# A gated cross-attention block in fp32: GpSimd's mixes in quarters behind VectorE's splits, and a new order around the last product

## The reference

```python
x = x + tanh(g_xattn) * attention(layernorm(x), ctx)   # 32 heads of 128, 8 key/value heads, RMS-normed q and k, out @ Wo
flat = layernorm(x)
probs = softmax(flat @ router_w.T + router_b); topv, topi = top_k(probs, 2)
w     = zeros(N, 8) with gates topv / sum(topv) at topi
h     = einsum('nd,erd->ner', flat, A)                 # 8 experts of rank 16
x = x + tanh(g_ffn) * einsum('ner,eor->no', h * w[:, :, None], Bm) * 0.5
```

## Time and profile before

| | us |
|---|---|
| median of 3 runs (1689.0 to 1690.82) | 1689.81 |
| profiled execution | 1685.8 |
| its span | 1684.0 |
| TensorE busy | 1650.3 |
| VectorE busy | 1176.9 |
| GpSimd busy | 889.1 |
| ScalarE busy | 877.3 |

### The profile page before, as it was taken

One profiled execution on the slowest core, in us unless ns is written; L12 is line 12 of the kernel. 1 busy time (PEld: TensorE's weight loads), 2 busy tenths in 40 slices (PEclk: granted clock), 3 DMA queues, 4 the chain that ended last, 5 costly groups with the idle time before them and its releaser, 6 DMA issues.

```text
span 1684.0 us, 26179 instructions
## 1 busy us (share of the span) xinstructions
PE 1650.3 (98%) x9120; PEld 1470.7 (87%) x9120; DVE 1176.9 (70%) x2054; ACT 877.3 (52%) x1663; POOL 889.1 (53%) x700
## 2 busy tenths in 40 slices
PE   7999999999999999999999999999999999999997
PEld 6788888678888879999999999999999889999995
DVE  7788886677777752677677777776766777556676
ACT  5545554544544431566666666666666666443432
POOL 1344443134434420777777777777776455563131
PEclk9999999999999999999999999999999999999999
DMA  5567778736566647556666666655556566687551
GB/s 200 157 171 235 232 207 249 194 112 188 151 180 164 159 161 235 173 166 208 197 213 198 198 204 189 191 190 180 182 171 205 187 215 218 229 281 248 222 178 58
DMA packets 238503, 323.87 MB, mean 192 GB/s; under 512 B 53300, under 2 KB 193396, under 8 KB 233380
## 3 DMA queue, kind: packets, MB, share of 16 engines
q1 hardware_dynamic: 237796, 315.65, 60.3%
q10 hardware_dynamic: 576, 6.55, 1.0%
HBM read 212.18 MB, written 109.97 MB: 191 GB/s over the span
## 4 chain that ended last, share of the span: by engine, by line
PE 89%; DVE 6%; ACT 3%; issue 2%; DMA 0%; POOL 0%; DVEq 0%; SPq 0%; ACTq 0%; POOLq 0%
PE bank L991 26%; PE bank L993 25%; PE bank L992 25%; PE bank L1129 5%; PE bank L1096 2%; PE bank L1025 1%; PE bank L1335 1%; DVE wo_lo L2024 1%; DVE mx L2004 1%; DVE at_lo L2026 1%; ACT pr L1611 1%; ACT w_hi L1427 1%; PE bank L1346 0%; DMA wr<-Wkv 0%; DVE pT_lo L1998 0%
## 5 line engine op out<-in xcount | busy, mean ns | idle before, releaser
L911 POOL TENSOR_SCALAR pr<-pr,rr 100x461 f32<-100x461 f32 x256 | 371.1, 1457 | 162.1 <-DVE rr L2019 162.1
L991 PE MATMUL bank<-w_hi,a_hi 128*128 128x512 f32 (+1 forms) x856 | 341.2, 399 | 11.0 <-DVE a_lo L1794 8.5
L993 PE MATMUL bank<-w_hi,a_lo 128*128 128x512 f32 (+1 forms) x856 | 335.2, 392 | 0.0
L992 PE MATMUL bank<-w_lo,a_hi 128*128 128x512 f32 (+1 forms) x856 | 334.3, 391 | 0.0
L1611 ACT ACTIVATE pr<-bank,nm,rq 100x461 f32<-100x461 f32 x256 | 188.7, 737 | 156.7 <-DVE nm L2010 155.0
L2004 DVE TENSOR_REDUCE mx<-bank 100x1 f32<-100x461 f32 x256 | 161.4, 631 | 78.5 <-PE bank L993 75.2
L865 POOL TENSOR_TENSOR msk<-ssk,epst 128x4 f32<-128x4 f32 (+1 forms) x60 | 22.9, 382 | 348.4 <-DVE ssk L1825 348.4
L991 PEld LDWEIGHTS bank<-w_hi,a_hi 128*128 128x128 f32 (+1 forms) x856 | 157.8, 184 | 48.4 <-issue 9.6
L993 PEld LDWEIGHTS bank<-w_hi,a_lo 128*128 128x128 f32 (+1 forms) x856 | 157.6, 184 | 38.4
L991 PE MATMUL bank<-xT_hi,wq_hi 128*128 128x400 f32 x512 | 188.3, 368 | 0.7 <-issue 0.7
L992 PEld LDWEIGHTS bank<-w_lo,a_hi 128*128 128x128 f32 (+1 forms) x856 | 158.0, 185 | 34.7
(11 more groups left out here) (159 smaller groups left out, 3556.1 us busy)
## 6 DMA issues: line engine op xcount, KB each, us to landing
kT_d<-kst SPq DMA_DIRECT2D x56, 512.0 KB, 5.6
v_d<-vst SPq DMA_DIRECT2D x56, 512.0 KB
kT<-kT_d SPq DMA_DIRECT2D x64, 361.0 KB, 4.5
kvr<-ctxT SPq DMA_DIRECT2D x44, 512.0 KB, 5.9
wq_raw<-Wq SPq DMA_DIRECT2D x32, 512.0 KB, 5.8
tb<-Wo SPq DMA_DIRECT2D x16, 1024.0 KB, 8.5
wt_d<-tb SPq DMA_DIRECT2D x16, 1024.0 KB, 7.8
wo_raw<-wt_d SPq DMA_DIRECT2D x16, 1024.0 KB, 7.4
```

What stands on the lines that cost most here:

```text
L911: pool.tensor_scalar(pr[0:NQ, u % 2, i], pr[0:NQ, u % 2, i], rr[0:NQ, i:i + 1], None, ALU.mult).then_inc(p_done, 1)
L991: pe.matmul(o, lh, rh, start=start, stop=False, skip_group_check=more)
L992: pe.matmul(o, lh, rl, start=False, stop=False, skip_group_check=more)
L993: return pe.matmul(o, ll, rh, start=False, stop=stop, skip_group_check=more)
```

## The change

GpSimd's three mixes become three sets of four instructions of 400 columns. Ahead of each set stands a wait for the split of a chunk (17, 18 and 19), and the counts of `mix_done` follow (3 becomes 12, 4 becomes 13). TensorE's c0 and d0 stand behind turn_y(3), ahead of the last product's last halves. For that c takes banks 4 and 0 and d takes 5 and 1, batch 7 has a tile of its own for `x1` (so it needn't wait for the end of batch 3), `halves_to` counts all first halves before the second ones, and the load of batch 7's input stands ahead of the store of batch 2. VectorE does d0's residual and two of the last four additions ahead of the routing's top, and a1's residual ahead of batch 3's gates.

```diff
+        x1_last = at("x1_last", RAW + 8 * KB, [P, D])
 def out_bank(t, half):
-            return ((4, 0), (5, 1), (4, 5), (0, 1))[t - TB][half] if t >= TB else 4 + half
+            return ((4, 0), (5, 1), (4, 0), (5, 1))[t - TB][half] if t >= TB else 4 + half
+        def x1_of(t):
+            return x1_last[:] if t == B - 1 else x1[:, t % 4]
 def halves_to(t, half):
-            return 1 + ((0, 0), (1, 0), (2, 0), (0, 1), (1, 1), (2, 1), (3, 0), (3, 1)).index((t - TB, half))
+            return 1 + t - TB + TB * half
 SyncE
             next_res(2)
+            next_res(3)
             store(2)
-            next_res(3)
 GpSimd
             pool.wait_ge(oT_dve, 10)
             pool.wait_ge(oT_act, 6)
-            pool.tensor_tensor(oT_late[:, first], oT_late[:, first], oT_early[:, second], ALU.add).then_inc(mix_done, 1)
-            pool.tensor_tensor(oT_early[:, second], oT_early[:, second], oT_late[:, second], ALU.add).then_inc(mix_done, 1)
-            pool.wait_ge(mix_done, 2)
-            pool.tensor_tensor(oT_late[:, second], oT_late[:, second], oT_late[:, first], ALU.add).then_inc(mix_done, 1)
+            pool.wait_ge(wo_lo_done, split_after(FIRST_OF[P4] + 1))
+            for c in range(GQ):
+                pool.tensor_tensor(oT_late[:, c], oT_late[:, c], oT_early[:, GQ + c], ALU.add).then_inc(mix_done, 1)
+            pool.wait_ge(wo_lo_done, split_after(FIRST_OF[P4] + 2))
+            for c in range(GQ, C):
+                pool.tensor_tensor(oT_early[:, c], oT_early[:, c], oT_late[:, c], ALU.add).then_inc(mix_done, 1)
+            pool.wait_ge(wo_lo_done, split_after(FIRST_OF[P4] + 3))
+            pool.wait_ge(mix_done, 2 * GQ)
+            for c in range(GQ, C):
+                pool.tensor_tensor(oT_late[:, c], oT_late[:, c], oT_late[:, c - GQ], ALU.add).then_inc(mix_done, 1)
 TensorE, turn_half
+                if t < TB + 2 and half == 0:
+                    pe.wait_ge(x1_done, 2 * TB)
+                if t >= TB + 2:
+                    pe.wait_ge(x1_done, 2 * TB + halves_to(t - 2, half))
+                if t == TB and half == 0:
+                    pe.wait_ge(oT_dve, 16)
+                    pe.wait_ge(mix_done, 3 * GQ + 1)
 TensorE, turn_y
                 if t > TB + 1:
-                    pe.wait_ge(x1_done, 2 * TB + halves_to(t, 1))
+                    pe.wait_ge(x1_done, 2 * TB + halves_to(TB + 3, t - TB - 2))
 TensorE, order
                 if n == 4 * GQ - 3:
                     turn_half(a, 0)
                     turn_half(b, 0)
+                if n == 4 * GQ - 2:
+                    turn_half(c, 0)
+                    turn_half(d, 0)
             last_half(0)
             last_half(1)
             low_rank(TB - 1)
-            turn_half(c, 0)
             last_half(2)
             last_half(3)
...
             low_rank(a)
-            turn_half(d, 0)
             turn_half(d, 1)
 VectorE, residual_half
-                    dve.wait_ge(x2_done, 2 * (t - 4) + 2)
+                    if t < B - 1:
+                        dve.wait_ge(x2_done, 2 * (t - 4) + 2)
 VectorE, last_accumulators(some) adds the banks in `some` only
 VectorE, order
             residual_half(b, 0)
+            residual_half(c, 0)
+            residual_half(d, 0)
+            last_accumulators((0, 1))
             route_top(TB - 1)
-            residual_half(c, 0)
-            last_accumulators()
+            last_accumulators((2, 3))
+            residual_half(a, 1)
             route_gates(a - 1)
-            residual_half(a, 1)
             residual_half(b, 1)
             final(a - 1)
             residual_half(c, 1)
             route(a)
-            residual_half(d, 0)
             residual_half(d, 1)
```

More of the change, by code:

```diff
@@ L960, in _ @@
                 chunk_sums(m)
-            first, second = (slice(0, C // 2), slice(C // 2, C))
             pool.wait_ge(oT_dve, 10)
             pool.wait_ge(oT_act, 6)
-            pool.tensor_tensor(oT_late[:, first], oT_late[:, first], oT_early[:, second], ALU.add).then_inc(mix_done, 1)
-            pool.tensor_tensor(oT_early[:, second], oT_early[:, second], oT_late[:, second], ALU.add).then_inc(mix_done, 1)
-            pool.wait_ge(mix_done, 2)
-            pool.tensor_tensor(oT_late[:, second], oT_late[:, second], oT_late[:, first], ALU.add).then_inc(mix_done, 1)
+            pool.wait_ge(wo_lo_done, split_after(FIRST_OF[P4] + 1))
[8 more added lines that the diff above has]
+                pool.tensor_tensor(oT_late[:, c], oT_late[:, c], oT_late[:, c - GQ], ALU.add).then_inc(mix_done, 1)
             for t in range(B):
@@ L1734, in norm @@
                     act.wait_ge(t2_done, t - 1)
-                act.activation(y[0:NQ, t % 2], x1[0:NQ, t % 4], ACT.Identity, bias=mv2[0:NQ, t, 3:4],
+                act.activation(y[0:NQ, t % 2], x1_of(t)[0:NQ], ACT.Identity, bias=mv2[0:NQ, t, 3:4],
                                scale=mv2[0:NQ, t, 1:2]).then_inc(y_done, 1)
@@ L2043, in accumulators @@
                 if o in (P4, P3):
-                    dve.wait_ge(mix_done, 3)
+                    dve.wait_ge(mix_done, 3 * GQ)
                 for n in (0, 1) if o in (P1, P7, P5, P2) else range(4):
@@ L2142, in residual @@
                 for n in range(2):
-                    dve.scalar_tensor_tensor(out=x1[0:NQ, t % 4, n * 512:(n + 1) * 512], in0=ps[out_bank(t, n)][0:NQ, :],
+                    dve.scalar_tensor_tensor(out=x1_of(t)[0:NQ, n * 512:(n + 1) * 512], in0=ps[out_bank(t, n)][0:NQ, :],
                                              scalar=gates_t[0:NQ, 0:1], in1=xr[t % 4][0:NQ, n * 512:(n + 1) * 512],
@@ L2147, in residual @@
                     dve.wait_ge(x1_done, 2 * t + n + 1)
-                    dve.bn_stats(bn6[0:NQ, t % 4, n], x1[0:NQ, t % 4, n * 512:(n + 1) * 512]).then_inc(st2_done, 1)
+                    dve.bn_stats(bn6[0:NQ, t % 4, n], x1_of(t)[0:NQ, n * 512:(n + 1) * 512]).then_inc(st2_done, 1)
                 dve.wait_ge(st2_done, 2 * t + 2)
@@ L2165, in residual_half, with last_accumulators @@
                     dve.bn_aggr(mv[0:NQ, t], bn6[0:NQ, t % 4]).then_inc(ag2_done, 1)
-            def last_accumulators():
-                dve.wait_ge(mix_done, 3)
-                for n in range(4):
+            def last_accumulators(some):
+                dve.wait_ge(mix_done, 3 * GQ)
+                for n in some:
                     dve.wait_ge(p3_done, n + 1)
```

2 lines of the change are left out of this document (1 added, 1 removed).

## The result

| | before | after |
|---|---|---|
| median of the timed runs, same chip | 1688.74 us (22 runs, 1686.23 to 1690.82) | 1691.68 us (22 runs, 1687.68 to 1697.11) |
| profiled execution | 1685.8 us | 1688.8 us |
| its span | 1684.0 us | 1687.0 us |

The ratio after to before is 1.0017, 95% interval 1.0009 to 1.0024: 1.5 to 4.1 us slower, where 1.8 us faster were forecast. The forecast of 1688.0 us started from 1689.81, the median of three runs; that of 22 runs is 1.1 us lower. The prediction was wrong, and the median lies outside its range.

A forecast was written before the change was run, and what follows sets the result against it. TensorE, busy 98% of the span, bounds the kernel, so only its queue gaps and the tail count. -3.0 (stalls) + 1.68 (hw) - 0.44 (d0) = -1.8 us, put on the median 1689.81: 1688.0 us, range 1685.8 to 1690.1.

The forecast's parts named there:

- Step 1: Quarter mixes behind the splits of chunks 17 to 19 remove TensorE's stalls: -3.0 us, bounds -3.0 and -1.0.
- chunk 19's weights land at 1538.3: Landing time taken between 1536.2 and 1539.64; chunk 19's split then ends at 1544.4, and TensorE wants it at 1546.0.
- no sooner than before (1539.64): Upper end for chunk 19's weights, if the 16 engines were simply full; the split's end at 1545.7 still just holds.
- the third rival: Stalls only partly gone, chunk 19's weights later than 1540 or a set over a split: +0.2 us, 1690.0; chance 0.12.
- Steps 2 and 3: c0, d0 ahead of the last halves: product 0.5 us later, tail 0.44 shorter; batch 7's input loaded sooner, no cost.
- Step 4: Two additions ahead of the routing's top on VectorE: a1's last transpose starts at 1650.27 for 1650.72, -0.45 us.
- Step 5: a1's residual ahead of batch 3's gates: `turn_h(3)` at 1653.45, 1.68 us later, and `low_rank(a)` later by +1.68.
- upper bound of +2.3: Tail's loss from the later `hw` if the low clock also lasts through c1 and `turn_y(a)`, adding 0.6 us.
- The fourth rival: Tail takes back more than the mixes give, low clock through batch 4's `low_rank`: +1.2 us, 1691.0; chance 0.07.

The follow-up runs named there:

- experiment 3: Small loads ahead of chunk 19 moved: on mixes alone, all late 1.0002, rows spread 0.9979, load gated 1.0006, `AR` and `BmT` late 0.9985; before, rows spread 0.9997.
- mixes alone: The kernel before with GpSimd's quarter mixes and their waits alone, the tail in its old order; 1690.59 us, ratio 0.9999.
- The changed kernel with the rows spread: The changed kernel with the four input-row loads put one behind each of the loads of chunks 20 to 23; 1685.86 us, ratio 0.9978.
- that with the gates first too: The changed kernel with input-row loads spread behind chunks 20 to 23 and batch 3's gates ahead of a1's residual; 1684.63 us, ratio 0.9971.
- mixes alone with the rows spread: The kernel before with the quarter mixes and the four input-row loads one behind each of chunks 20 to 23; 1685.59 us, ratio 0.9979.
- tail alone: The changed kernel with the three old mixes of 1600 columns, keeping only the edits around the last product; 1690.81 us, ratio 1.0008.
- gap filled: The changed kernel with seven useless fp32 identity products on TensorE ahead of its wait for chunk 19; 1691.16 us, ratio 1.0008.
- the kernel with the wait filled: The changed kernel with 14 useless matmuls between a1's transposes and `turn_h(3)`, in the wait for `hw`; 1688.31 us, ratio 1.0001.

## Why the prediction was wrong, step by step

**Step 1, the mixes: the right mechanism with one term mis-sized.** Splits at 2.29 and 1.82 us, four quarters in 4.05 us and no stall ahead of chunks 17 and 18 came as written, and the loads were issued when forecast (1526.27 when the 1.95 us of later start are taken off; forecast 1526.2). The term that failed is "chunk 19's weights land at 1538.3", with the bound "no sooner than before (1539.64)" taken as the worst. They landed at 1541.6 on the old time scale, 2.0 us *later than before though issued 3.4 sooner*. The old 9.94 us had been read as the price of one load under load; it was what remained of a queue with 2.7 MB of small loads in it after 3.4 us more of it had drained, by experiment 3. This is the third rival ("chunk 19's weights land later than 1540"), which had 0.12; each us beyond its limit costs one, as it said. The step was worth -3.0 + 1.7 = -1.3 us, 1.7 being the difference in mid with and without the input rows in the way (137.05 and 135.30). Two runs show both sides: 15.63 us with all six loads ahead (mixes alone), at most 7.2 with the four rows spread.

The Trainium skill, DMA: Bandwidth & Descriptors, section "Queues, rings and completion order", says that the loads of one issuing engine share one ring on each of the 16 DMA engines, and that these take descriptors in the order of the ring. The traces agree (holding back what is behind chunk 19 left 15.2 us, taking away what is ahead made it 12.39), and a term built on it, bytes ahead over the rate, would have been nearer than a duration carried over, but only with the rate of the rows: by the windows some 3.7 MB were still to come at the issue in the changed kernel, an estimated 9 us at 400 GB/s and 14 at 260.

**Steps 2 and 3, halves and input rows: right.** c0 and d0 ahead cost the mid 0.42 us (135.30 for 134.88) for 0.5 forecast, and the residual of d0 started at 1644.95, right behind that of c0, and never waited for `xr`.

**Step 4: right.** a1's last transpose starts 1.02 us behind the last product for 1.97 before; less the 0.5 us by which that product moved, -0.45.

**Step 5: right in its mechanism, short in the first profile.** `turn_h(3)` starts 4.16 us behind the last product (forecast 1653.45 - 1649.25 = 4.20). Batch 4's `low_rank` follows at 11.53 for 10.45 forecast, since the low clock lasted over the transposes too: +2.8 in the forecast's terms, above its upper bound of +2.3. In the other five profiles it follows at 10.13 to 10.58. The fourth rival's `low_rank` at half the clock didn't come (2.10 us in all six). Over six profiles the tail averages 36.2 us for 36.0 forecast. What the step had no chance to see is that its start, 35.25 us, was a short one: a typical tail before is 36.1, so that against it the tail loses about 0.1 us, and not the 0.74 (36.0 - 35.25) that the forecast comes to. That its size came out is in part luck.

**The sum.** With step 1 as measured the forecast would have been -1.8 + 1.7 = -0.1 us, no change. The runs say 1.5 to 4.1 us slower, so some 1.6 to 4.2 us beyond that are in no single profile. One part shows in numbers: the mean granted clock of the 22 executions is 0.9963, of before's 109 in the experiments 0.9973, and among the 22 a clock lower by 0.001 goes with 1.2 us. That is 1.2 us. The changed kernel with the rows spread, and that with the gates first too, have 0.9981 and a standard deviation of 0.9 us, for 2.7 of after, which fits falls of the clock that come in some executions only; mixes alone with the rows spread has 0.9975 and 2.0 us though, so it isn't the gap alone.

Where the rest lies stays open. The six profiles of after average 1688.7 us, some 3 us under the median of its 22 runs, and by their mids (137.4 on average for before's 137.8) and tails (36.2 for 36.1) the changed part would be a little shorter than before. Four profiles of other variants do show long times, 1693.22 (mixes alone), 1694.35 (tail alone), 1689.60 (mixes alone, rows spread) and 1693.24 us (gap filled). In them P5's copies start between 1516.3 and 1518.0 us, in the other sixteen between 1510.65 and 1514.9, and all up to there is code that no kernel here changes. In three of the four one collision is to be seen, here in mixes alone with the rows spread: an earlier `wo_lo` lies beside GpSimd's sums of operands and takes 5.34 us, where the other profiles have 2.29 to 2.95, and TensorE stands still for `pT_lo` behind it:

```profile
1441.12 5.34 DVE L2036 TENSOR_TENSOR wo_lo<-wo_raw,wo_hi 128x2048 fp32r<-128x2048 f32 x1 [1.23 <-ACT wo_hi L1641]
```
```profile
1446.99 0.45 PE L996 MATMUL bank<-pT_hi,vv 120*128 120x400 f32 x1 [2.88 <-DVE pT_lo L2003]
```

How often each kernel meets it isn't known, and whether it is behind the long times among after's 22 runs isn't shown.

## What to carry to other kernels

A load that is issued sooner doesn't land sooner when its queue is the limit: count the bytes issued ahead of it and divide by the rate of that mixture, in place of carrying its old time from issue to landing over. When a stall is taken away, ask which prefetch was living off it, and spread small loads that are wanted late over the large ones. A wait on TensorE can cost the products behind it as well, when the granted clock falls to half: it did behind the 2.83 us of the tail in all nine profiles that have them, but not behind the 2.63 us of chunk 19 in the kernel with the wait filled. So profile the kernel before more than once, to see on which of the two sides the chosen execution lies.

## What the runs showed of the hardware

- The 100-row input tiles of 400 KB hold the 16 DMA engines at a share of 0.98 to 1.09 while only 240 to 270 GB/s move; without them it is 375 to 438 GB/s. The 6.3 MB from chunk 18's operands to chunk 19's weights took 21.9 us before (1517.73 to 1539.64) and 23.9 us after (1519.68 to 1543.56), though they are the same bytes. Chunk 20's operands were in flight for the last 7 us of it, but holding them back changed little (15.2 us for 15.63). With them held back the share was 0.64, 0.70 and 0.29 in the last three windows of 2 us before chunk 19's weights were in (1536 to 1542), so part of the 16 engines had nothing left while others still worked on them. How the loads are spread over the engines may then count beside the sum of the bytes; no run tests it. Why the closer spacing made the same bytes slower wasn't found.
- The third set of mixes, beside chunk 20's split, took 7.70 us for 4.05, and the `at_lo` there 2.67 for 1.82: with quarters it is GpSimd that loses most (3.65 us), and the split 0.85, where whole mixes had added 2.0 to 3.4 us to a split.
- The same program (before) had a tail of 35.25 and of 36.80 us; the sixteen products of batch 4's `low_rank` took 2.10 us in the one and 3.71 in the other.
- Useless matmuls in a wait of 2.83 us gave back 1.7 us of tail against the mean of six profiles, 2.6 against the first.
